# Local attention: the inverse norm of a query row as scale of its exponential instead of a multiplication of the queries

## The reference, cut to what matters

```python
q = l2norm(q) * qs
k = l2norm(k) * ksc
q = q * cos * scale + rotate_half(q) * sin * scale
inv = 1.0 / scale
k = k * cos * inv + rotate_half(k) * sin * inv
...
sim = jnp.einsum('bhwie,bhwje->bhwij', bq, bk2) * QK_SCALE
sim = jnp.where(mask, -jnp.finfo(sim.dtype).max, sim)
attn = jax.nn.softmax(sim, -1)
```

## Time and profile before

| | us |
|---|---|
| median of 3 runs | 3656.92 |
| lowest and highest | 3654.7, 3661.24 |
| the profiled execution, its own time | 3656.62 |
| its span | 3654.8 |
| PE busy (share of the span) | 3031.7 (83%) |
| DVE | 2072.7 (57%) |
| ACT | 2013.6 (55%) |
| POOL | 1595.3 (44%) |

### The profile page before, as it was taken

One profiled execution on the slowest core, in us unless ns is written; L12 is line 12 of the kernel. 1 busy time (PEld: TensorE's weight loads), 2 busy tenths in 40 slices (PEclk: granted clock), 3 DMA queues, 4 the chain that ended last, 5 costly groups with the idle time before them and its releaser, 6 DMA issues. The chain is left out here.

```text
span 3654.8 us, 79424 instructions
## 1 busy us (share of the span) xinstructions
PE 3031.7 (83%) x29522; PEld 1910.8 (52%) x29522; DVE 2072.7 (57%) x3872; ACT 2013.6 (55%) x5960; POOL 1595.3 (44%) x1845
## 2 busy tenths in 40 slices
PE   4987888888888888788888888888889998897796
PEld 1545665465545664566545664666455653463352
DVE  2746665567646664666557654666332323474573
ACT  3446776577747774677657764777412223355343
POOL 0416664466626662666356652666121200230340
PEclk8899999999989999999989998999957989799797
DMA  2000000000000000000000000000000000000000
GB/s 84 2 10 24 0 0 25 8 1 0 0 32 1 0 0 32 1 0 0 25 8 1 0 1 32 1 0 0 25 24 1 1 1 0 1 2 1 1 2 12
DMA packets 4956, 32.82 MB, mean 9 GB/s; under 512 B 1041, under 2 KB 1937, under 8 KB 2833
## 3 DMA queue, kind: packets, MB, share of 16 engines
q1 hardware_dynamic: 4752, 29.96, 2.3%
HBM read 28.91 MB, written 1.05 MB: 8 GB/s over the span
## 5 line engine op out<-in xcount | busy, mean ns | idle before, releaser
L983 POOL TENSOR_TENSOR l_qk<-l_ta,l_tb 128x256 f32<-128x256 f32 x768 | 548.0, 736 | 561.7 <-DVE l_tb L1042 561.7
L902 ACT ACTIVATE l_pr<-st,l_mn 128x128 f32<-128x128 f32 x1536 | 547.8, 383 | 277.5 <-DVE l_mn L1030 277.5
L649 DVE TENSOR_REDUCE mrow<-ring 128x2 f32<-128x512 f32 x512 | 328.2, 685 | 298.1 <-PE ring L491 284.4
L771 PE MATMUL ring<-l_wa,l_xs 128*128 128x512 f32 x768 | 399.9, 645 | 102.0 <-DVE l_xs L1025 57.8
L617 POOL TENSOR_SCALAR qmr<-q_all,cf 128x256 fp32r<-128x256 f32 x128 | 115.9, 924 | 827.8 <-SPq L447 401.3
L1041 DVE TENSOR_TENSOR l_ta<-ring,l_tab 128x512 f32<-128x512 f32 x384 | 263.8, 687 | 319.8 <-ACT l_sq L911 319.7
L776 PE MATMUL ring<-l_wa,l_xs 128*128 128x256 f32 x768 | 227.5, 420 | 259.3 <-DVE l_tb L1042 237.5
L602 ACT ACTIVATE pt<-st 128x512 f32<-128x512 f32 x384 | 210.6, 599 | 415.6 <-PE st L519 415.6
L999 POOL TENSOR_TENSOR l_qk<-l_qk,l_rn 128x512 f32<-128x512 f32 x384 | 398.9, 1059 | 87.6 <-DVE l_rn L1061 87.6
L990 POOL TENSOR_TENSOR l_pr<-l_pr,l_rs 128x512 f32<-128x512 f32 x384 | 391.2, 1040 | 50.4 <-DVE l_rs L1051 50.4
L902 ACT ACTIVATION_READ_ACCUMULATOR l_pr<-st,l_mn 128x1 f32 x1536 | 340.2, 221 | 0.0
(11 more groups left out here) (220 smaller groups left out, 5989.6 us busy)
## 6 DMA issues: line engine op xcount, KB each, us to landing
l_wa<-in_wa SPq DMA_DIRECT2D x7, 2048.0 KB, 9.2
l_wf<-in_wf SPq DMA_DIRECT2D x6, 580.5 KB, 4.3
w<-in_w SPq DMA_DIRECT2D x1, 2752.0 KB, 15.6
cf<-in_cf SPq DMA_DIRECT2D x1, 1253.0 KB, 7.5
x<-in_xT SPq DMA_DIRECT2D x1, 1024.0 KB, 5.0
ctxT<-in_ctxT SPq DMA_DIRECT2D x1, 1024.0 KB, 9.5
pad_r<-in_pad_r SPq DMA_DIRECT2D x1, 1024.0 KB, 17.3
mask_q<-in_mask_q SPq DMA_DIRECT2D x1, 1024.0 KB, 4.9
```

Source lines behind the costliest of these rows:

```text
L649: dve.tensor_reduce(mrow[b % 2][:, t, j, 2 * p:2 * p + 2], bank_of(f"R{r}").rearrange("p (h k) -> p h k", h=2), AX.X, ALU.max).then_inc(ri ...
L771: mm = pe.matmul(bank, t.xs[:, j * P:(j + 1) * P], t.wa[:, k % GROUPS * C:(k % GROUPS + 1) * C], start=True, stop=True)
L902: ins = act.activation(t.pr[:, u, hh, c, tile, :], g.st[:, rows_bank(k) + hh, x * P:(x + 1) * P], ACT.Exp, scale=-1.0, bias=t.mn[:, u, hh, ...
L983: ins = pool.tensor_tensor(halves[0][:, :, x], halves[1][:, :, x], halves[2][:, :, 1 - x], ALU.add)
```

## The change

The queries are no longer multiplied by their inverse norms. Instead:

- POOL multiplies only the keys, so `normalise` is one instruction instead of two, and PE's `turn` waits for the sum of the rotation products for the queries and for that instruction for the keys.
- The query tables lose their minus sign and the mask band becomes negative; DVE takes maxima into a new small tile `t.mx`, and behind both reductions two new scalar_tensor_tensor instructions write the bias, −(maximum × inverse norm), into `t.mn`.
- The exponentials take the inverse norm of their row from memory as their scale, which was the constant −1 before.
- The inverse norms are kept for four groups (`t.rn` gets a dimension `GROUPS`), because they are read until the exponentials are done.

```diff
-    for n, s in (("lq", -8.0 * sc), ("lk", 1.0 / sc)):
+    for n, s in (("lq", 8.0 * sc), ("lk", 1.0 / sc)):
...
-            band.append(np.where((q - k >= 0) & (q - k <= WIN), 0.0, -MASKED))
-    b["negband"] = np.concatenate(band, axis=1)
+            band.append(np.where((q - k >= 0) & (q - k <= WIN), 0.0, MASKED))
+    b["rowband"] = np.concatenate(band, axis=1)
...
             def turn(N, k):
                 for x in range(2):
-                    pe.wait_ge(qk_normed, 2 * N + x + 1)
+                    if x:
+                        pe.wait_ge(k_normed, N + 1)
+                    else:
+                        pe.wait_ge(ab_summed, 2 * N + 2)
...
             def exps(N, k, hh):
                 u = k % 2
-                act.wait_ge(mins_ready, 2 * N + hh + 1)
+                act.wait_ge(bias_ready, 2 * N + hh + 1)
                 for x in range(4):
                     c, tile = divmod(x, 2)
                     ins = act.activation(t.pr[:, u, hh, c, tile, :],
-                                         g.st[:, rows_bank(k) + hh, x * P:(x + 1) * P], ACT.Exp, scale=-1.0,
+                                         g.st[:, rows_bank(k) + hh, x * P:(x + 1) * P], ACT.Exp,
+                                         scale=t.rn[:, k % GROUPS, tile, 2 * c + hh:2 * c + hh + 1],
                                          bias=t.mn[:, u, hh, x:x + 1], accum_out=t.ps[:, u, hh, x:x + 1])
...
-                for x in range(2):
-                    at = k % GROUPS * C + x * GQ
-                    part = t.qk[:, :, at:at + GQ].rearrange("p t (h k) -> p t h k", k=LHD)
-                    pool.tensor_tensor(part, part, t.rn[:, :, 4 * x:4 * x + 4].unsqueeze(3).broadcast_to([P, 2, 4, LHD]),
-                                       ALU.mult).then_inc(qk_normed, 1)
+                at = k % GROUPS * C + GQ
+                part = t.qk[:, :, at:at + GQ].rearrange("p t (h k) -> p t h k", k=LHD)
+                pool.tensor_tensor(part, part, t.rn[:, k % GROUPS, :, 4:8].unsqueeze(3).broadcast_to([P, 2, 4, LHD]),
+                                   ALU.mult).then_inc(k_normed, 1)
...
-            def minima(N, k):
+            def maxima(N, k):
+
                 dve.wait_ge(rows_ready, N + 1)
                 for hh in range(2):
-                    dve.tensor_reduce(t.mn[:, k % 2, hh, :],
+                    dve.tensor_reduce(t.mx[:, hh, :],
                                       g.st[:, rows_bank(k) + hh, :].rearrange("p (x k) -> p x k", x=4),
-                                      AX.X, ALU.min).then_inc(mins_ready, 1)
+                                      AX.X, ALU.max).then_inc(max_ready, 1)
+                for hh in range(2):
+                    dve.wait_ge(max_ready, 2 * N + hh + 1)
+                    mx, mn = (x.rearrange("p (c t) -> p c t", c=2) for x in (t.mx[:, hh, :], t.mn[:, k % 2, hh, :]))
+                    rq = t.rn[:, k % GROUPS, :, hh:4:2].rearrange("p t c -> p c t")
+                    dve.scalar_tensor_tensor(out=mn, in0=mx, scalar=-1.0, in1=rq, op0=ALU.mult,
+                                             op1=ALU.mult).then_inc(bias_ready, 1)
...
-        self.rn = tmp("l_rn", [P, 2, 8], F32)
+        self.rn = tmp("l_rn", [P, GROUPS, 2, 8], F32)
...
+        self.mx = tmp("l_mx", [P, 2, 4], F32)
```

More of the change, by code:

```diff
@@ L737, in local_attention @@
     ab_summed, n2_ready, guess, rn_ready = g.sem("l_ab_summed"), g.sem("l_n2_ready"), g.sem("l_rnorm_guess"), g.sem("l_rnorm_ready")
-    qk_normed, turned, turn_copied = g.sem("l_qk_normed"), g.sem("l_qk_turned"), g.sem("l_turned_copied")
-    rows_ready, mins_ready, exps_done = g.sem("l_rows_ready"), g.sem("l_minima_ready"), g.sem("l_exps_done")
+    k_normed, turned, turn_copied = g.sem("l_k_normed"), g.sem("l_qk_turned"), g.sem("l_turned_copied")
+    rows_ready, max_ready, bias_ready, exps_done = g.sem("l_rows_ready"), g.sem("l_maxima_ready"), g.sem("l_bias_ready"), g.sem("l_exps_done")
     recip_ready, p_normed = g.sem("l_reciprocals_ready"), g.sem("l_probs_normed")
@@ L796, in rows @@
                     for w in range(2):
-                        band = B_AT["negband"] + w * SEQ
+                        band = B_AT["rowband"] + w * SEQ
                         pe.matmul(g.st[lane[w], rows_bank(k) + hh, :].rearrange("p (c k) -> p c k", c=2),
@@ L928, in values_to_sbuf, with inverse_norms @@
                                ACT.Copy).then_inc(ring_act, 1)
-            def inverse_norms(N):
+            def inverse_norms(N, k):
                 act.wait_ge(n2_ready, N + 1)
@@ L933, in inverse_norms @@
                 act.wait_ge(aown, N + 1)
-                act.activation(t.rn[:, :, :], t.lnv[:, :, :], ACT.Exp, scale=-0.5,
+                act.activation(t.rn[:, k % GROUPS, :, :], t.lnv[:, :, :], ACT.Exp, scale=-0.5,
                                bias=g.f("lnoff", 1)).then_inc(guess, 1)
@@ L956, in step @@
                     values_to_sbuf(N + 2, k + 2)
-                    inverse_norms(N + 2)
+                    inverse_norms(N + 2, k + 2)
                 if k >= 1:
@@ L1051, in reciprocals, with refine @@
                 dve.reciprocal(t.rs[:, k % 2, :, :], t.ps[:, k % 2, :, :]).then_inc(recip_ready, 1)
-            def refine(N):
-                r, n2, w = t.rn[:, :, :], t.n2[:, :, :], t.nw[:, :, :]
+            def refine(N, k):
+                r, n2, w = t.rn[:, k % GROUPS, :, :], t.n2[:, :, :], t.nw[:, :, :]
                 dve.wait_ge(guess, N + 1)
@@ L1070, in step @@
                 if 0 <= k < STEPS:
-                    minima(N, k)
+                    maxima(N, k)
                 if k + 2 < STEPS:
@@ L1080, in step @@
                 if k + 2 < STEPS:
-                    refine(N + 2)
+                    refine(N + 2, k + 2)
                 if k + 4 < STEPS and k % GROUPS == 1:
```

## The result

| | before | after |
|---|---|---|
| median, us (4 runs each) | 3659.08 | 4005.94 |
| lowest and highest | 3654.7, 3662.76 | 3994.36, 4015.2 |
| ratio, 95% interval | | 1.0947 [1.0908, 1.0986] |
| profiled execution, span | 3654.8 | 4013.4 |

The account below looks back on a forecast made before the run. A chain of waits, not a full engine, bounds it: per step a PE loop of 9.89 us and a POOL loop of 9.62. 3656.6 + 239 (without the clock) + 157 (clock) = 4052.6, say 4050; range 3880 to 4115.

Parts of the forecast that it names:

- The bias: Bias operations behind both maxima, ahead of the exponentials: the first exponential starts 0.70 us later in each step.
- both loops: Two chains of waits set a group step: one through PE, 9.89 us, one through POOL's division, 9.62 us.
- The scale from memory: Exponentials reading their scale from memory: 0.095 us each, four on the PE loop (+0.38), eight on the POOL loop (+0.76).
- POOL's halved multiplication: Multiplying only keys on POOL: gain 0 in the steady step, hidden under the exponentials; −6 us at the depths' starts.
- not slower: Rival: POOL's queue sets the step, so the lost 1.04 us comes off each, giving 3457 us; chance 0.03.
- The sum without the clock: All steps of six depths at full clock: 22 × 1.19 + 10 × 1.46 per depth, less 6, +239 us.
- The POOL loop: Waits through POOL's division and DVE's refining operations: 9.62 us per step, 11.08 after the change, then deciding.
- The clock: PE's gap ahead of its third projection grows from 1.48 to 2.56 us; half the steps fall to 1.2 GHz, +157 us.
- Its argument: PE's 2.56 us gap lies midway between gaps that kept (1.89) and lost (3.32) the clock, so half the steps fall.
- The rival that the clock stays up: PE keeps its clock despite the longer gap ahead of its third projection, giving 3896 us; chance 0.20.

Follow-up runs that it names:

- the filler: Four matmuls whose result nobody reads, added in PE's gap of each step from a depth's third on; changed kernel 3907.92 us, kernel before 3660.39.
- a_warm: The changed kernel plus four unread matmuls in PE's gap of each step from a depth's third on; 3907.92 us, ratio 1.0678.
- a_const_warm: a_warm with the constant 0.125 as scale of the exponentials in place of the inverse norm from memory; 3777.54 us, ratio 1.0334.
- b_mem_scale: The kernel before with the exponentials' scale −1 read from a column in memory; 3823.45 us, ratio 1.0472; with the filler 3790.95, 1.0387.
- a_const: The changed kernel with the constant 0.125 as scale of the exponentials, without extra matmuls; 3901.92 us, ratio 1.0686.
- the control: The kernel before with the same four unread matmuls in PE's gap; 3660.39 us, ratio 1.0011.
- b_turn_recip: The kernel before with PE's query transposes ahead of the third projection, and reciprocals and POOL's division between the projections' two halves; 3584.52 us, ratio 0.9812.

## Why the prediction was right, point by point

- **The bias, +0.70 on both loops, 128 us.** Right. The first exponential starts 0.67 later, and the bias alone costs 117 with the filler. Its instruction takes 0.16 (forecast 0.17), and the key multiplication does not hold it.
- **The scale from memory, 0.095 per exponential.** Right: 0.44 instead of 0.345 from start to start, also where it is the only edit. The Trainium skill, ScalarE: Activation LUTs, section "What ACT_TABLE_LOAD costs", has 93 ns per pointer operand; the runs agree, for the second one as for the first. The forecast's share of it is (22 × 0.49 + 10 × 0.76) × 6 = 110 us, measured 130. Some 15 of the rest are one step per depth: from the reduction of step 30 to that of step 31 it takes 12.47 to 12.51 in five depths of a_warm and 9.48 in the sixth, in a_const_warm 8.75. The 9.48 is what the forecast's 0.76 gives, so the 3.0 on top belong to the clock and not to the operand. In the profile after, in order of time on PE, the clock falls just there:

```profile
660.58 1.11 PE L791 MATMUL st<-cf,l_qk 128*128 128x128 f32 x4 [2.53 <-ACT l_pr L905]
...
666.12 2.07 PE L854 MATMUL ring<-l_o,l_wa 128*128 128x256 f32 x4
```

- **POOL's halved multiplication: 0 in the steady step, −6 at the starts.** The 0 holds, and "not slower" is refuted: POOL's queue set no step by this instruction. The 1.0 at a depth's start is there as well: from a depth's first projection to its first reduction it takes 13.31 to 13.35 in all six depths, where before it took 14.32 or 14.33 in three and 15.32 to 15.57 in the others; what holds those three back further was not looked at. The first reduction is at 293.52 in both profiles only because the weights landed 0.97 later in the profile after. Of the two rows, the first is of the kernel before, the second of the one after:

```profile
279.20 3.78 PE L771 MATMUL ring<-l_wa,l_xs 128*128 128x512 f32 x4 [13.15 <-DMA l_wa<-in_wa]
```

```profile
280.17 3.77 PE L771 MATMUL ring<-l_wa,l_xs 128*128 128x512 f32 x4 [13.89 <-DMA l_wa<-in_wa]
```

The times between depths are equal all the same: the stretch from a depth's last reduction to the next first projection grew from 62.5 to 64.3 on the mean of five, as much as the start lost. That the last step's bias and exponentials, which lie in it, are the reason is not shown.
- **The sum without the clock, +239.** Bias and scale with the filler give 117 + 130 = 247, of which a part is falls that the filler left. Shift steps grew by 1.35 where 1.46 was forecast. The POOL loop decides at full clock, as forecast, but its step of 11.08 is in part luck: the steps of a_warm mostly take 11.08, 11.36 and 10.96 in turn, 11.13 on the mean, and two errors of the one figure for all of them, 0.12 up and 0.28 down, nearly cancel.
- **The clock, +157 (0 to 315).** The mechanism is right, its size was off: this is the term that makes the 44 us. It measured 98, with falls left in both; the granted clock was 0.89, forecast 0.85. A fall made 68 of the 132 regular steps longer, and seven shift steps, where the forecast has 87 of 174. The 68 cost 1.36 each against the same steps of a_warm, not 1.81. The price was too high because it took the stretch from L830 to L851 as slow throughout (4.53 instead of 2.61). In the two falls read here it was not: in the profile after, the same stretch takes 3.13 in the fall shown above (546.80 to 549.93), and in the fall at 336.25 it takes 2.60 (339.86 to 342.46): by then the clock was back, and only L776 and the transposes had been slow. The second interval of each depth, the first shift step, took 14.83 in all six, before 11.17 to 13.44, which is 8 us in all more than the 1.46 that was forecast. It takes 14.83 in a_warm too, whose filler does not run there, so the 98 do not hold it.
- **Its argument failed.** "2.56 lies midway between a row that kept the clock and one that lost it" treats one gap as the cause. b_mem_scale loses the clock behind 1.88 and keeps it behind 1.89, and a_const loses it at 2.1. The rival that the clock stays up is refuted by a_warm, and the Trainium skill's warning of longer gaps only (TensorE: Matmul & The Clock Gate, section "Why this matters for your kernels") is not borne out here: the filler, which shortens every gap, gave 98 and 124 us back. That nearly half of the steps fell was therefore luck. What makes one step fall and the next not was not settled.

The three measured terms, 117 + 130 + 98 = 345, meet the 347 us by construction, since each is the difference of two neighbours in one chain of kernels, and the 2 us left are the control's. Another order gives the clock another share: with the bias alone the filler gives back 124 (a_const), with the scale alone 32 (b_mem_scale).

## What to carry to other kernels

Write down each loop of waits with its length before costing an edit: an instruction that leaves a queue with slack (POOL here) gains nothing, and 0.1 us on an instruction that runs eight times in the loop costs over 100 us. When an edit lengthens a loop, PE idles longer in it and may lose its clock: price that as a term of its own, and test it with filler matmuls in the gap, with the same filler in the kernel before as control. Put a small operation that others wait for directly behind its own input, not behind its sister's (73 to 79 us here).

## What was not expected of the hardware

- PE dropped to 1.2 GHz in a kernel whose steady gaps are only 1.6 to 2.0 us, some steps after others with the same gaps at 2.4 GHz (b_mem_scale, granted clock 0.92 over 290 to 2600 us).
- A DVE instruction with two SBUF inputs waited out a POOL instruction (0.50 instead of 0.16 us, the pair 1.10 instead of 0.28), and with one of its inputs in PSUM it did not: 160 to 164 ns in all 384 cases, against up to 507. The Trainium skill, SBUF — State Buffer, section "Who interferes with whom", puts this interference down to both inputs being in SBUF, and the runs agree. A one-input tensor_scalar of 16 elements was held too (1.04 in b_turn_recip, against 0.21 when free); the same section lists tensor_scalar among the operations that can take the shared ports.
